# Embedding, attention and experts on one core: the token rules in two spans

## What is computed

```python
h = einsum('bsd,bsde->bse', base_embeddings[ids], rule_transform[token_rules[ids]])   # 100 rules of 64x64
x = layernorm(h)
q, k = x @ Q[head], x @ K[head]                    # 8 heads, 32 wide
attn = softmax(q @ k.T / sqrt(64)); h = h + sum over heads of (attn @ x) @ VO[head]
x = layernorm(h); logits = x @ Wg + bg + bias      # 8 experts, the best 2, softmax weights
h = h + sum over experts of weight * (relu(x @ W1 + b1) @ W2 + b2)
```

## Time and profile of the kernel before

| | us |
|---|---|
| runs | 674.33, 678.36, 679.65 |
| profiled execution, its time | 682.98 |
| its span in the trace | 681.2 |
| PE busy (matmul) | 499.3 |
| PE loading weights | 260.3 |
| DVE busy | 413.1 |
| ACT busy | 266.5 |
| POOL busy | 221.3 |

### The profile page before, as it was taken

How to read it: one execution, slowest core, us unless ns; L and a number is a source line. 1 busy time by engine, 2 the same in 40 slices (tenths; PEclk the granted TensorE clock), 3 DMA queues, 4 the chain that set the end, 5 groups by cost and what they waited for, 6 DMA issues and landing times.

```text
span 681.2 us, 8447 instructions
## 1 busy us (share of the span) xinstructions
PE 499.3 (73%) x2368; PEld 260.3 (38%) x2368; DVE 413.1 (61%) x966; ACT 266.5 (39%) x503; POOL 221.3 (32%) x366
## 2 busy tenths in 40 slices
PE   0101047833462999999999999999999999997580
PEld 0100025731131444544544544544554454446240
DVE  6328302425563686888969969868867766536521
ACT  1000003411011565546555564565565356661350
POOL 5773770027700000130224224134133133336424
PEclk9999997985555999999999999999999899996876
DMA  8410004621905244340440430421232000000000
GB/s 244 155 25 8 26 27 114 168 55 32 206 4 124 64 94 94 71 99 20 94 95 1 93 83 22 93 59 45 60 89 48 1 9 2 9 1 9 0 9 8
DMA packets 21195, 41.88 MB, mean 61 GB/s; under 512 B 5856, under 2 KB 12704, under 8 KB 21088
## 3 DMA queue, kind: packets, MB, share of 16 engines
q1 hardware_dynamic: 17072, 33.80, 20.9%
q10 hardware_dynamic: 1008, 4.33, 2.1%
q0 software_dynamic: 3072, 3.22, 1.9%
HBM read 8.26 MB, written 7.60 MB: 23 GB/s over the span
## 4 chain that ended last, share of the span: by engine, by line
PE 59%; DVE 12%; POOL 12%; issue 7%; DMA 3%; ACTq 2%; ACT 2%; another core or an unknown queue 2%; SPq 1%; POOLq 0%; DVEq 0%
PE bank L896 17%; PE bank L885 10%; PE bank L871 8%; POOL etok L382 5%; POOL emb_sorted L390 5%; PE bank L857 5%; PE bank L838 4%; PE bank L798 4%; PE bank L832 2%; DVE mx L712 2%; ACTq L462 2%; PE bank L833 2%; DVE vtmp L730 2%; POOL acc L413 2%
## 5 line engine op out<-in xcount | busy, mean ns | idle before, releaser
L712 DVE TENSOR_REDUCE mx<-bank 128x1 f32<-128x512 f32 x256 | 171.5, 687 | 69.7 <-PE bank L885 57.9
L470 ACT ACTIVATE prob<-bank 128x512 f32<-128x512 f32 x256 | 138.7, 596 | 66.8 <-PE bank L871 66.4
L413 POOL TENSOR_TENSOR acc<-vtmp 128x256 f32<-128x256 f32 x64 | 49.0, 766 | 280.4 <-DVE vtmp L747 189.9
L896 PE MATMUL bank<-prob,xa 128*64 128x512 f32 x512 | 139.9, 625 | 0.0
L885 PE MATMUL bank<-ks,qs 96*128 96x512 f32 x256 | 122.3, 482 | 22.5 <-issue 12.8
L885 PEld LDWEIGHTS bank<-ks,qs 96*128 96x128 f32 x256 | 50.7, 198 | 138.6 <-issue 115.6
L871 PE MATMUL bank<-qs,ks 97*128 97x512 f32 x256 | 88.1, 426 | 12.7 <-DMA qs<-negm 12.7
L500 ACT ACTIVATE hid<-bank,stay 128x512 f32<-128x512 f32 x64 | 43.2, 686 | 67.6 <-PE bank L833 67.6
L453 ACT COPY eT<-bank 64x256 f32<-64x256 f32 x42 | 15.4, 367 | 116.6 <-PE bank L788 116.3
L871 PEld LDWEIGHTS bank<-qs,ks 97*128 97x128 f32 x256 | 44.0, 193 | 31.9 <-DMA qs<-negm 13.8
L413 POOL TENSOR_TENSOR acc<-acc 128x128 f32<-128x128 f32 (+1 forms) x128 | 50.3, 393 | 10.0
(11 more groups left out here) (134 smaller groups left out, 641.4 us busy)
## 6 DMA issues: line engine op xcount, KB each, us to landing
qs<-qk_h SPq DMA_DIRECT2D x64, 128.0 KB
ks<-qk_h SPq DMA_DIRECT2D x56, 128.0 KB
qs<-qk_l SPq DMA_DIRECT2D x32, 128.0 KB
ks<-qk_l SPq DMA_DIRECT2D x28, 128.0 KB
emb_sorted<-zrow ACTq DMA_DIRECT2D x3, 896.0 KB
y_sorted<-y_out SPq DMA_DIRECT2D x21, 128.0 KB, 2.4
e_in<-emb_sorted SPq DMA_DIRECT2D x10, 256.0 KB, 2.9
r_sb<-in_rules SPq DMA_DIRECT2D x1, 1600.0 KB, 14.5
```

The costliest lines, as they stand in the source:

```text
L413: nc.gpsimd.tensor_tensor(a[:, at:at + width], src[:, 0:width], src[:, width:2 * width], ALU.add).then_inc(S["pool_chain"], 1)
L470: nc.scalar.activation(prob[:, step % NPROB, u % 2, :], bank[u % NST][:], ACT.Exp, scale=SC).then_inc(S["exp_done"], 1)
L712: V.tensor_reduce(mx[:, u // 16, u % 16:u % 16 + 1], bank[3 + n % 2][:], AX.X, ALU.max).then_inc(S["mx_done"], 1)
L896: last = M(bank[5][64 * hh:64 * hh + 64, :], xa[:, b * J + ut, :], prob[:, (16 * b + k) % NPROB, hh, :], start=(ut == 0), stop=(ut == J - 1))
```

## The change

The tokens are split at batch 2: `SPAN` is chunks 0 to 7 and chunks 8 to 31. Each span has its own ranks, counts, starts and slots, its own `emb_sorted` and `y_sorted`, and its own set of tiles: 15 groups for the first span (`NG[0]`), 19 for the second.

- POOL gathers 18 chunks, scatters the first span, gathers the other 14 chunks, brings batch 0 back, scatters 8 chunks of the second span, brings batch 1 back, scatters the other 16. It then issues the second span's loads and stores itself (`load_pair`, `store_group`, direct transfers), and brings batches 2 to 7 back after the last store. `values` (the copy to `xa`) of batches 0 and 1 lies between these.
- PE does the first span's 15 groups as before. The second span's 19 groups become auxiliary tasks `rT` (transposes) and `rule` (products) in the two ring banks: one group a step from (-1, 9) to (-1, 15), two a step from (0, 0) to (0, 5), the last `rule` at (0, 6). ACT does both of their copies.
- DVE looks at quarters 2 and 3 between the first span's copies, does the starts, the slots of quarter 1 and the tile rules of span 1 before LN(0), and the slots of quarters 2 and 3 at (-2, 9). LN(1) starts at (-1, 3), LN(2) at (0, 8), LN(3) at (0, 12); in b = 0 two pieces a step.
- The projections of batch 2 move from (0, 5) to (0, 8) to (0, 13) to (0, 15), with their transposes at (0, 12).
- On SP the weights wait for the first quarter's gathers, the rules go ahead of them, and in b = -1 and 0 `max_row(b+1, 0)` goes ahead of the stacks of batch b + 2. On ACT the second span's zeros also wait for the first quarter.
- Buffers: `xn` becomes a ring of two batches with a separate `xn2`, `xa` a ring of three; `hid`, `vtmp` and `acc` lie in `r_sb`, `etok` in `ctxT`, the weights to be split and the zeros under `qs` and `ks`. DVE and POOL get waits for those rings.

The diff, cut to its core:

```diff
+    FIRST = 2 * J
+    SPAN = ((0, FIRST), (FIRST, NC))
+    NG = [-(-(NR + ((hi - lo) * 128 - 1) // TS) // GT) for lo, hi in SPAN]
+    BASE = (0, NG[0])
+    TOTAL = NG[0] + NG[1]
+    PAIRS = [[g] if g + 1 == end else [g, g + 1] for base, n in zip(BASE, NG) for end in (base + n,)
+             for g in range(base, base + n, 2)]
...
+        X_AT = {(0, XT), (1, 10), (2, 12)} | {(nb, XT) for nb in range(3, B)}
+        R_AT = [(-1, 9 + g) for g in range(7)] + [(0, g // 2) for g in range(13)]
+
+        def proj_at(nb):
+
+            return {1: (11, 12, 13, 14), 2: (13, 14, 15, 15)}.get(nb, PROJ)
+
...
-            late = 6 if b == -1 else 0
-            if k == XT + late and 0 <= b + 2 < B:
+            if (b + 2, k) in X_AT:
                 todo.append(("xT", b + 2, 0))
-            if k - late in PROJ and 0 <= b + 2 < B:
-                todo.append(("proj", b + 2, PROJ.index(k - late)))
+            todo += [("proj", b + 2, i) for i in range(4) if 0 <= b + 2 < B and proj_at(b + 2)[i] == k]
...
+            for g in range(TOTAL - BASE[1] + 1):
+                if R_AT[g] == (b, k):
+                    todo += [("rT", BASE[1] + g, 0)] if g < NG[1] else []
+                    todo += [("rule", BASE[1] + g - 1, 0)] if g else []
...
+            i = n >= NP0
+            g, at_ = PAIRS[n][0] - BASE[i], 2 * n % NE_IN
+            w = len(PAIRS[n])
+            eng.dma_start(e_in[:, at_:at_ + w, :], es[i][:, g:g + w, :]).then_inc(e_in_sem[i][n % (NE_IN // 2)], 16)
...
             sp.dma_start(ids[:, 0, :], ids_in).then_inc(S["ids_in"], 16)
             sp.dma_start(cst[:], consts).then_inc(S["cst_in"], 16)
+            sp.dma_start(r_sb[0:D, :], rules).then_inc(S["rules_in"], 16)
+            sp.wait_ge(e_got[0], 16 * QC)
             sp.dma_start(stay[:], weights[:, 0:NSTAY]).then_inc(S["w_in"], 16)
-            sp.dma_start(load[:], weights[:, NSTAY:NSTAY + NLOAD]).then_inc(S["w_in"], 16)
-            sp.dma_start(r_sb[0:D, :], rules).then_inc(S["rules_in"], 16)
...
-            sp.wait_ge(S["scattered"], 16 * NC)
-            for gp in range(NGP + AHEAD):
...
+            sp.dma_start(load, weights[:, NSTAY:NSTAY + NLOAD]).then_inc(S["w_in"], 16)
+
+            sp.wait_ge(S["scattered_0"], 16 * FIRST)
+            for n in range(NP0 + AHEAD):
+                if n < NP0:
+                    if n >= NE_IN // 2:
+                        sp.wait_ge(S["eT_ps"], PAIRS[n - NE_IN // 2][-1] + 1)
+                    load_pair(sp, n)
+                for g in PAIRS[n - AHEAD] if n >= AHEAD else ():
+                    sp.wait_ge(S["y_ok"], g + 1)
+                    store_group(sp, g)
...
             sp.wait_ge(S["ones_ok"], 1)
+            sp.wait_ge(S["zeroed_1"], 16 * 4)
...
@@ -361,10 +405,12 @@
                     stack(b + 1, 3)
                 if 0 <= b < B:
                     max_row(b, 1)
+                if b in (-1, 0):
+                    max_row(b + 1, 0)
                 if 0 <= b + 2 < B:
                     stack(b + 2, 0)
                     stack(b + 2, 1)
-                if 0 <= b + 1 < B:
+                if 1 <= b and b + 1 < B:
                     max_row(b + 1, 0)
                 if 0 <= b + 2 < B:
                     stack(b + 2, 2)
...
+                    if c % QC == 0:
+                        pool.wait_ge(S["pos_ok"], c // QC + 1)
+                    nc.gpsimd.indirect_dma_start(emb_sorted[i], bass.IndirectOffsetOnAxis(ap=pos[:, c:c + 1], axis=0),
+                                                 etok[:, c, 0:D], None).then_inc(S[f"scattered_{i}"], 16)
+                    if c == 2:
+                        nc.gpsimd.memset(mark[:], 0.0).then_inc(S["scatters_issued"], 1)
...
+            def bring(i, b):
+
+                for c in range(b * J, (b + 1) * J):
+                    nc.gpsimd.indirect_dma_start(hbuf[:, c, :], None, y_sorted[i],
...
+            def values(b):
+
+                pool.wait_ge(S["xn_ready"], b + 1)
+                if b >= XAR:
+                    pool.wait_ge(S["pv_done"], 16 * (b + 1 - XAR))
+                nc.gpsimd.tensor_copy(xa[:, b % XAR, :, 1:D], xn[:, b % XNR, :, 0, 1:D]).then_inc(S["xa_ready"], 1)
...
+            fetch(range(FIRST + 10))
+            pool.wait_ge(S["zeroed_0"], 16 * 3)
+            place(0, range(FIRST))
+            fetch(range(FIRST + 10, NC))
             nc.gpsimd.memset(xa[:], 1.0).then_inc(S["xa_set"], 1)
             pool.wait_ge(S["xa_set"], 1)
-            pool.wait_ge(S["zeroed"], 16 * 3)
-            for c in range(NC):
-                if c % QC == 0:
-                    pool.wait_ge(S["pos_ok"], c // QC + 1)
-                nc.gpsimd.indirect_dma_start(emb_sorted, bass.IndirectOffsetOnAxis(ap=pos[:, c:c + 1], axis=0),
-                                             etok[:, c, 0:D], None).then_inc(S["scattered"], 16)
-                if c == NC - 8:
...
-            for q in range(4):
-                pool.wait_ge(y_out_sem[q], 16 * len(range(q, NG, 4)))
-            for b in range(B):
-                for c in range(b * J, (b + 1) * J):
-                    nc.gpsimd.indirect_dma_start(hbuf[:, c, :], None, y_sorted,
-                                                 bass.IndirectOffsetOnAxis(ap=pos[:, c:c + 1], axis=0)).then_inc(y_loaded[b], 16)
+            for g in range(NG[0] - 4, NG[0]):
+                store_sent(pool, g)
+            bring(0, 0)
+            pool.wait_ge(S["zeroed_1"], 16 * 4)
+            place(1, range(FIRST, FIRST + QC))
+            bring(0, 1)
+            values(0)
+            place(1, range(FIRST + QC, NC))
+            pool.wait_ge(S["scattered_1"], 16 * (NC - FIRST))
+            for n in range(NP0, len(PAIRS) + AHEAD):
+                if n < len(PAIRS):
+                    if n >= NE_IN // 2:
+                        pool.wait_ge(S["eT_ps"], PAIRS[n - NE_IN // 2][-1] + 1)
+                    load_pair(pool, n)
+                if n == NP0 + 1:
+                    values(1)
+                for g in PAIRS[n - AHEAD] if n >= NP0 + AHEAD else ():
+                    pool.wait_ge(S["y_ok"], g + 1)
+                    store_group(pool, g)
+            for g in range(TOTAL - 4, TOTAL):
+                store_sent(pool, g)
+            for b in range(2, B):
+                bring(1, b)
...
             for b in range(-2, B + 1):
-                if b + 2 < B:
-
-                    pool.wait_ge(S["xn_ready"], b + 3)
-                    c = slice((b + 2) * J, (b + 3) * J)
-                    nc.gpsimd.tensor_copy(xa[:, c, 1:D], xn[:, c, 0, 1:D]).then_inc(S["xa_ready"], 1)
+                if 2 <= b + 2 < B:
+                    values(b + 2)
...
-            flat = emb_sorted.rearrange("(z p s) d -> z p (s d)", z=3, p=128)
-            for i in range(3):
-                act.dma_start(flat[i], zrow[:]).then_inc(S["zeroed"], 16)
+            for i, parts in enumerate((3, 4)):
+                if i:
+                    act.wait_ge(e_got[0], 16 * QC)
+                flat = emb_sorted[i].rearrange("(z p s) d -> z p (s d)", z=parts, p=128)
+                for z in range(parts):
+                    act.dma_start(flat[z], zrow[:, 0:NG[i] * 4 * D // parts]).then_inc(S[f"zeroed_{i}"], 16)
...
-            for g in range(NG):
+            for g in range(NG[0]):
...
+                        if kind == "rT":
+                            act.wait_ge(S["eT_ps"], ab + 1)
+                            act.wait_ge(S["y_ps"], ab - 1)
+                            for r in range(2):
+                                ins = nc.scalar.copy(eT[0:D, ab % 2, r * 256:(r + 1) * 256], ring(a)[64 * r:64 * r + 64, 0:256])
+                            ins.then_inc(S["eT_ok"], 1)
+                        if kind == "rule":
+                            act.wait_ge(S["y_ps"], ab + 1)
+                            store_sent(act, ab - 4)
+                            nc.scalar.copy(y_out[:, ab % 4, :], ring(a)[0:TS, :]).then_inc(S["y_ok"], 1)
...
-            for q in range(NQ):
+
+            def look(i, q):
+
                 c0, c1 = q * QC, (q + 1) * QC
+                lo = SPAN[i][0]
                 rf, rt = rule[:, 0, c0:c1], rule[:, 1, c0:c1]
...
+                yield
+                V.tensor_tensor(oh[:, c0 - lo:c1 - lo, :], ramp_f[:, 0:NR].unsqueeze(1).to_broadcast([128, QC, NR]),
                                 rf.unsqueeze(2).to_broadcast([128, QC, NR]), ALU.is_equal).then_inc(S["oh_ok"], 1)
-                link(V.tensor_tensor(same[:, :, 0:c1], rule[:, 0, 0:c1].unsqueeze(1).to_broadcast([128, QC, c1]),
-                                     rf.unsqueeze(2).to_broadcast([128, QC, c1]), ALU.is_equal))
-                link(V.tensor_tensor(same[:, :, c0:c1], same[:, :, c0:c1], earlier, ALU.mult))
-                link(V.tensor_reduce(rank[:, c0:c1], same[:, :, 0:c1], AX.X, ALU.add))
+                dve.wait_ge(S["oh_ok"], q + 1)
+                yield
...
+                link(V.tensor_reduce(rank[:, c0:c1], same[:, :, 0:w], AX.X, ALU.add))
                 link(V.tensor_copy(rule_i[:, c0:c1], rf))
...
```

(64 more changed lines are left out.)

242 lines of the change are left out of this document (131 added, 111 removed).

## The result

| | kernel before | changed kernel |
|---|---|---|
| device time, median | 676.35 us (674.30 to 679.65, 4 runs) | 652.14 us (651.78 to 654.25, 4 runs) |
| ratio to before, 95% interval | | 0.9644 (0.9592 to 0.9696) |
| span of the profiled execution | 681.2 us | 650.4 us |
| PE busy | 499.3 us (73%) | 517.2 us (80%) |
| POOL busy | 221.3 us | 239.0 us |

The changed kernel was 3.6% faster here, and 3.0% (0.9704, 0.967 to 0.9739) when it ran again on another chip. On a further one it brought nothing (0.9997); the last experiments are about that.

What follows compares the result with a forecast made beforehand. Up to about 217 us a front chain over all 32 chunks leaves PE mostly idle; then PE is full. Batch 1 34.3 us earlier, less 8 given back, makes -26.3: 652 from the median 678.4, range 634 to 668.

Steps and rivals of the forecast that it cites:

- The stage of 15 groups: First span's rule products on PE: fifteenth copy 26.2 us after the first transpose, plus 1 for DVE's rank steps.
- The ranking: DVE ranks the second span before LN(0): 13 us, ending at 84, deciding over the gathered data at 80.6 by 3.
- The two losses: PE waits 7 us for LN(2) in batch 0 and about 6 for SP's queue in batch 1, each plus 2 of clock.
- T + 21.1: Landing of batch 1's second row maxima behind SP's transfers, T being batch 1's start; PE needs them at T + 16.1.
- Rival A: The main forecast: most of the 70 us lead at the front is given back by waits; 643 to 661 us, chance 0.50.
- Rival B: Waits for LN(2) and SP's queue don't appear because PE gets there later: 15 us less, 637 us; chance 0.25.
- rival C: POOL's direct transfers pace the second span's rule products: 678 us at 3.0 us an issue, 709 at 4; chance 0.07.
- Rival D: PE's clock stays at 1.2 GHz up to batch 1: about +25 us on the main forecast, 677 us; chance 0.05.
- Rival E: The front does better, with quicker gathers and cold groups: up to 10 us less, 642 us; chance 0.13.
- my 26.3: Net gain over the whole kernel: 34.3 us ahead at batch 1's start, less 8 given back there.
- Its 4% for slower: Chance 0.04 that the changed kernel is slower, beside 0.92 for faster by over 1% and 0.04 for within 1%.

Runs made afterwards that it cites:

- the last experiments: Changed kernel again on a chip with pauses: 682.0 us, ratio 0.9997; beside it, denser rule products plus eased SP queue in batch 1: 665.0 us, 0.9762.
- experiment 4: Changed kernel with each store of a second-span rule product group split into two half-size transfers by POOL; ratio to the kernel before 0.9727, span 654.9 us.
- 5: The changed kernel itself, unedited, run again on another chip; ratio to the kernel before 0.9704, span 650.5 us.
- experiment 7: Changed kernel with second-span rule products started at (-1,12), three a step, then two a step to (0,3); 637.6 us, ratio to the kernel before 0.9456.
- experiment 6: Changed kernel with second-span rule products packed two a step in steps 9 to 15 of batch -1 and 0 to 2 of batch 0; ratio 0.9573.
- 8: Changed kernel with batch 1's second row maxima before the stacks of heads 4 to 7 of batch 2, projections of batches 3 and 4 moved; ratio 0.9641.
- 9: Changed kernel with max_row(1, 1) before the last six transfers only, SP's landing waits deferred, batch 3's projections at steps 8, 9, 10, 12; ratio 0.9878, chip with pauses.
- Experiment 2: Kernel before with one edit: batch 0's first row maxima sent on SP before the stack transfers of batch 1; ratio to the kernel before 0.9844.
- experiment 3: Changed kernel with SP sending the 1.4 MB of weights at the start, not held for the first eight gathers; ratio to the kernel before 0.9738, span 659.1 us.

## Why the prediction came out right, and where it did not

The predicted time was 652 and the range 634 to 668; measured were 652.14. The chain that it followed is the one in the trace, but two errors cancel in the number, so that it came out to the microsecond is luck.

| step | predicted | measured |
|---|---|---|
| first gathers seen; first scatter; first transposes | 18.5; 29.5; 43.8 | 18.15; 29.36; 43.75 |
| first transposes to 15th copy | 26.2 + 1 | 22.8 |
| 15th copy to LN(0) | 13 | 11.1 |
| LN(0) to last projection | 14.3 | 14.0 |
| last projection to first rT (scatters, load) | 30.7 | 30.5 |
| PE's wait there | 10 | 9.7 |
| first rT to first attention product | 22.5 | 23.2 |
| batch 0, with groups and LN(2)'s wait | 73.7 | 74.3 |
| of it the wait; the clock after it | 7; 2 | 7.3; about 2 |
| batch 1 begins, to before | -34.3 | -39.9 |
| given back to SP's queue and the clock | 8 | 8.9 |
| sum, to the profiled execution | -26.3 | -31.0 at the ruler, -30.8 at the end |

**The stage of 15 groups was mis-sized,** 27.2 us for 22.8. I took it whole from before, where its first seven microseconds ran at a clock of 0.55. Here PE came to it at a clock of 1.00 (44 to 50 us); in experiments 4, 5 and 7 it had 0.56 to 0.72 there, and LN(0) came at 79.0 to 80.8 us. So 3.4 of the 4.4 us are the clock of the first groups, and 1 is what I had added for DVE's rank steps, which cost nothing. The bound from the row of full clock, 15 times 1.44, stood ready and was not used.

**The ranking was estimated at 13 us**, and it was not alone in deciding: with 11.1, DVE's idle time before LN(0) is 0.41 us, ended by the gather. Ranks and gather are equal, where the prediction had DVE last by 3 us.

**The two losses were right in place and in size**, and the experiments confirm each: packing the products earlier takes the first away (experiment 6), SP's order the second (8 and 9). Of the two reasons that the prediction gave for the second, what ended the wait was ACT's copy of batch 3's first projection (240.50 us), and not the row maxima from which its T + 21.1 was worked out; the two lie within a microsecond of each other. Rival A said that most of the lead is given back by waits: of the net 46 us between LN(0) and the end 28 are waits and their clock (9.7 at the head of PE's queue, 9.3 and 8.9 at the two dents), the rest is added work less the wait of 12.3 that went. Rival B, that they don't appear, is refuted. So is rival C: POOL's direct transfers took 0.61 us a store and 0.73 to 0.77 a load, under the 0.94 us of an indirect one, and doubling the stores moved the stage by 0.3 us at most (experiment 4). The Trainium skill's rule in DMA: Bandwidth & Descriptors, "Issuing engine by pattern", gives plain loads and stores to Sync; the rows show no price for going against it here (POOL's stores landed in 2.6 us, SP's in 2.9), though the same transfers were not tried from SP. Rival D did not come: the clock was 0.72 from 122 to 145 us and 1.00 from 145 to 180. Its sum does not add up either: 16 and 21 are 37, not about 25, and nothing says what takes off the rest. Rival E came in part: batch 1 began 5.6 us earlier than the sum had it, by the quicker front.

**The cancelling errors.** By trace the gain is 4.5 us larger than predicted. By time it is 24.2 (676.35 to 652.14), 2 smaller than my 26.3. The profiled execution of before lay 6.6 us above the median that the second measurement gave (and 4.6 above the one that the prediction had), that of after is its median. Experiment 2 shows where most of that may lie: 6.9 us between the last projection and the row maxima of the kernel before. A difference of two profiled executions carries that error, and I had subtracted a sum made on one from the median of others.

**What the prediction had no case for** is a chip on which the gain vanishes. Its 4% for slower had one mechanism each for POOL and for the clock; here PE, ACT and DVE pause together. The trace that it was worked out from may have had a first sign of it, the 6.9 us above.

## What to carry to other kernels

When a long front is cut into a short first part and a rest, cost the rest as tasks in the queues it is put into: of the net 46 us given back here, 28 were waits at the place chosen and the half clock behind them (10 at the head of PE's queue, 9 at LN(2), 9 on SP), and placing the rule products better won 15 us more (experiment 7). Ask of each moved task when its input comes, and put it behind the last work that doesn't need it. Try the small reordering that comes with a large change by itself: here it was 10 of the 24 us. And before a profiled execution is used as the base of a sum, compare its time with the median of the runs, and look for waits that nothing in it ended.

## What the runs showed of the hardware that was not expected

- On two chips PE, ACT and DVE paused, but for single steps, during long runs of indirect transfers on POOL (22 and 24 in a row, 1.25 us each), and went on 1 to 3 us after the last. The first pause cost 14 us, the second 16 to 19, together 31 of 650. On the other chips there was nothing of it in this kernel. The cause is open.
- PE ran 15 us at half clock while 100% busy, after one 5 us stretch at 76% (505 to 520 us of experiment 3, 7.8 us lost), and in other runs of the same schedule lost 1.6 us there or nothing. In the first run of the changed kernel PE was 75% busy for 5 us (495 to 500 us) and stayed at 1.00.
- A direct transfer issued by POOL took it 0.61 us (128 KB) and 0.73 to 0.77 us (256 KB), two halves of 64 KB 0.53 each.
